# LayerNorm statistics from sums taken in the residual additions and squares taken on ScalarE, transposed inputs from the host, and a new order on every engine, in a fused attention and feed-forward block

## The chip, the cores and the metric

The kernel runs on one core of a Trainium2 chip. The metric is the time of one execution on the device, in microseconds (us). Five engines work side by side, each through a list of its own, strictly in the order in which the program was written: TensorE (PE: matmuls and transposes), VectorE (DVE), ScalarE (ACT), GpSimd (POOL) and SyncE (SP, here only a queue that issues transfers). They wait for each other through semaphores.

## What is computed

One block on x of 2 sequences x 2048 tokens x 256 channels, all float32. First linear attention with 16 heads of 16 channels, then a feed-forward layer whose inputs and weights are rounded to a block format (32 neighbours share the exponent of the largest, with 3 bits of mantissa). A LayerNorm without weights follows each.

```python
qkv = x @ Wqkv.T + bqkv;  q, k, v = split(qkv)
q, k = elu(q * scale) + 1, elu(k * scale) + 1
ksum, kvsum = cumsum(k), cumsum(k * v)            # along the tokens
y = q * kvsum / clip(sum_of_head(q * ksum), 1e-3)
x = layernorm(x + y @ Wproj.T + bproj)            # first norm, over 256 channels
h = gelu(quant(x) @ quant(w_fc).T + b_fc)         # 1024 hidden
x = layernorm(x + quant(h) @ quant(w_proj).T + b_proj)   # second norm
```

## The kernel before

The 4096 tokens are cut into 8 chunks of 512 tokens (4 tiles of 128), numbered n = 0 to 7 with the two sequences in turn. Everything is written out by hand: for each engine there are small functions, one for each step of a chunk, and a list of calls that is that engine's order. Four steps of the lists are written as a function step(s), the first and the last chunks are written out. Nothing reorders at run time.

**Attention of a chunk.** x_sb holds the chunk with tokens on the partitions. PE transposes it through a bank of PSUM (transpose_x, L1106), ACT copies it to xT (copy_xT, L512), and PE projects (project, L1116) six times, for q, k and v with two halves c of the channels. A projection goes to one of the two banks abank[0] and abank[1]. ACT takes q and k through a Relu and an Exp (activate, L521 and L523), DVE adds and takes the maximum (feature, L782), multiplies k and v (multiply_kv, L789) and runs the two cumulative sums (sum_k L794, sum_kv L799). Only then is the bank free again. POOL multiplies q by the sums (L349, L353). PE sums by head (denominators, L1127), DVE takes the reciprocal, ACT widens it (widen_rec, L531), PE transposes it (L1135), DVE forms y (attention_out, L811), PE projects it out (project_out, L1146 and L1148), DVE adds x (residual_1, L815).

**First norm.** DVE reads r1 again with bn_stats, one instruction for each tile (L821), combines them with bn_aggr (L825), and takes the negative mean (L828) and the variance plus epsilon (L829). POOL raises that to the power -1/2 (L358) and multiplies by the mean (L360). ACT applies both (norm_1, L536).

**Feed-forward of a chunk.** DVE takes the largest of each 32 (x_exponents, L834), POOL scales and rounds (L365), DVE scales back (quantise_x, L758). A transposing transfer turns it (turn_xq on SP). PE multiplies by w_fc, two halves for each tile, into the banks hbank[0] and hbank[1] (up, L1182 and L1184), and ACT applies GELU (L527). DVE takes the maxima (h_exponents, L857, L750, L753), POOL rounds (round_h, L380), DVE scales back (quantise_h, L758), a transposing transfer turns it (turn_hq), PE multiplies by w_proj into the one bank dbank (down, L1189 and L1193), DVE adds (residual_2, L869). The second norm is as the first, and SP stores the chunk.

Attention of chunk n + 2 is mixed with the feed-forward of chunks n and n + 1. The weights are loaded, q and k parts of Wqkv are scaled, and all are transposed on PE and copied on ACT at the beginning; the feed-forward weights are rounded there too (w_exponents L766, round_w L390).

[...] Exp and Gelu are in different sets, and the compiler puts an ACT_TABLE_LOAD ahead of an activation whose set isn't the one loaded. Relu, Identity, Copy and Square need none.

## Time and profile before

| | |
|---|---|
| time, median of 3 | 276.79 us (276.34 to 281.1) |
| span of the profiled execution | 273.3 us |
| median less span | 3.5 us |
| PE busy | 240.0 us, 88% |
| DVE busy | 238.9 us, 87% |
| POOL busy | 155.0 us, 57% |
| ACT busy | 151.0 us, 55% |
| granted PE clock, mean | 0.982 |
| read from and written to HBM | 7.35 MB, 4.19 MB |

The time of the profiled execution is not known by itself; its span, from the first to the last instruction, is 3.5 us under the median of the timed runs, and that difference is what lies around the span. Busy time is the time in which an engine has at least one instruction under way, so overlaps of neighbours are counted once. A mean of one instruction counts them again: the step from the start of one to the start of the next is shorter than the duration.

### The profile page before, as it was taken

The page shows a single profiled execution, that of the slowest core. Times are in us where ns is not written, and L with a number is a line of the kernel's source. Part 1 is how long each engine was busy: PE and PEld are TensorE (multiplying, and loading weights), DVE is VectorE, ACT ScalarE, POOL GpSimd, SP SyncE. Part 2 cuts the span into 40 slices and gives each one's busy share as a digit, 9 for nine tenths or more (in the row PEclk, how much of TensorE's full clock was granted, in tenths as well). Part 3 has the DMA queues.
Part 4 walks back from the last instruction along what each step waited for, and adds up shares of the span by engine and source line. Part 5 has one row for each costly group of instructions (what it writes and reads, how often), then busy time and mean ns, then how long its engine had stood idle before and what let it go on. Part 6 is the DMA issues. An engine that isn't in the chain of part 4 may idle for free.

```text
span 273.3 us, 3668 instructions
## 1 busy us (share of the span) xinstructions
PE 240.0 (88%) x1204; PEld 143.4 (52%) x1204; DVE 238.9 (87%) x513; ACT 151.0 (55%) x246; POOL 155.0 (57%) x118
## 2 busy tenths in 40 slices
PE   7999889997999899989999899989999989838761
PEld 7546636653566446644656356644664455524340
DVE  1398997998998999899989999899989997978962
ACT  2663277745556851855475754685285646332823
POOL 1076466575376656476566737675647656655851
PEclk9999999999999999999999999999999997979997
DMA  6940020036202473227304490238224530642022
GB/s 155 365 97 2 0 78 1 2 70 155 46 0 38 77 193 42 38 39 190 81 0 77 114 160 0 41 64 205 38 36 44 110 83 0 65 90 78 0 79 77
DMA packets 49474, 20.70 MB, mean 76 GB/s; under 512 B 38960, under 2 KB 49200, under 8 KB 49456
## 3 DMA queue, kind: packets, MB, share of 16 engines
q1 hardware_dynamic: 47824, 20.20, 32.7%
q10 hardware_dynamic: 1632, 0.27, 0.6%
q8 instruction: 10, 0.16, 0.3%
q14 instruction: 8, 0.07, 0.1%
HBM read 7.35 MB, written 4.19 MB: 42 GB/s over the span
## 4 chain that ended last, share of the span: by engine, by line
DVE 56%; PE 25%; DMA 8%; POOL 4%; issue 3%; ACT 2%; SPq 1%; ACTq 0%; POOLq 0%; DVEq 0%
DVE vbank L857 12%; PE abank L1116 8%; DVE hq L758 7%; DVE vbank L821 6%; PE dbank L1193 5%; DVE kvsum L799 4%; DMA h<-in_L_ffn_w_fc_dram 4%; POOL h_round L380 3%; PE hbank L1184 3%; DVE r L815 3%; DVE r L869 3%; DVE vbank L834 3%; DMA xqT<-xq 2%; DVE h_pow L750 2%; DVE kf L782 2%
## 5 line engine op out<-in xcount | busy, mean ns | idle before, releaser
L1116 PE MATMUL abank<-xT,WqkvT 128*128 128x512 f32 x176 | 81.6, 599 | 3.6 <-DVE kf L782 2.2
L380 POOL TENSOR_TENSOR h_round<-h,h_inv 128x1024 f16<-128x1024 f32 x32 | 66.5, 2079 | 31.2 <-DVE h_inv L753 28.5
L527 ACT ACTIVATE h<-hbank 128x512 f32<-128x512 f32 x64 | 36.7, 595 | 51.3 <-PE hbank L1184 51.0
L1116 PEld LDWEIGHTS abank<-xT,WqkvT 128*128 128x128 f32 x176 | 31.1, 190 | 36.2 <-issue 23.7
L857 DVE TENSOR_REDUCE vbank<-h 128x32 f32<-128x1024 f32 x32 | 39.1, 1221 | 1.6 <-ACT h L527 1.5
L349 POOL TENSOR_TENSOR qk<-qf,ksum 128x512 f32<-128x512 f32 x16 | 23.5, 1469 | 29.4 <-DVE ksum L794 18.6
L1184 PE MATMUL hbank<-w_fcT,xqT 128*128 128x512 bf16 x128 | 39.1, 387 | 0.0
L521 ACT ACTIVATE expz<-abank,zbias_neg 128x512 f32<-128x512 f32 x30 | 20.6, 687 | 31.9 <-PE abank L1116 31.4
L1193 PE MATMUL dbank<-w_prT,hT 128*128 128x256 bf16 x256 | 34.4, 279 | 1.9 <-DMA hT<-hq 1.3
L1148 PE MATMUL bbank<-WprojT,y 128*128 128x256 f32 x128 | 32.0, 380 | 0.0
L1193 PEld LDWEIGHTS dbank<-w_prT,hT 128*128 128x128 bf16 x256 | 25.2, 100 | 9.5 <-issue 3.3
L1182 PE MATMUL hbank<-bias_rows,ones_k 128*128 128x512 bf16 x64 | 25.1, 392 | 2.1 <-DMA xqT<-xq 0.9
L358 POOL TENSOR_TENSOR rstd<-vareps,minus_half 128x4 f32<-128x4 f32 (+1 forms) x18 | 17.4, 966 | 15.9 <-DVE vareps L829 15.8
L758 DVE TENSOR_TENSOR hq<-h_round,h_pow 128x1024 bf16<-128x1024 f16 x32 | 21.8, 685 | 3.5 <-POOL h_round L380 3.5
L1148 PEld LDWEIGHTS bbank<-WprojT,y 128*128 128x128 f32 x128 | 21.8, 190 | 5.2
L353 POOL TENSOR_TENSOR num<-qf,kvsum 128x512 f32<-128x512 f32 x16 | 20.9, 1324 | 5.0 <-DVE kvsum L799 5.0
L365 POOL TENSOR_TENSOR x_round<-x,x_inv 128x1024 f16<-128x1024 f32 (+1 forms) x9 | 15.5, 1723 | 13.7 <-DVE x_inv L753 13.7
L821 DVE BATCH_NORM_STATS2 vbank<-r 128x6 f32<-128x256 f32 x64 | 22.7, 420 | 0.3
L794 DVE TENSOR_TENSOR_SCAN ksum<-vbank,ksum,kf 128x512 f32<-128x512 f32 x16 | 20.5, 1279 | 0.3
L523 ACT ACTIVATE expz<-expz 128x512 f32<-128x512 f32 x32 | 20.1, 630 | 0.9
L799 DVE TENSOR_TENSOR_SCAN kvsum<-vbank,kvsum,kv 128x512 f32<-128x512 f32 x16 | 20.2, 1262 | 0.0
L1189 PE MATMUL dbank<-bias_rows,ones_k 128*128 128x256 bf16 x32 | 9.1, 283 | 12.6 <-DVE r L869 12.6
(102 smaller groups left out, 357.4 us busy)
## 6 DMA issues: line engine op xcount, KB each, us to landing
x_sb<-in_L_attn_x_dram SPq DMA_DIRECT2D x8, 512.0 KB, 3.9
out_dram<-o_sb SPq DMA_DIRECT2D x7, 512.0 KB, 3.5
h<-in_L_ffn_w_fc_dram SPq DMA_DIRECT2D x1, 1024.0 KB, 9.6
h<-in_L_ffn_w_proj_dram SPq DMA_DIRECT2D x1, 1024.0 KB, 11.1
Wqkv_sb<-in_L_attn_Wqkv_dram SPq DMA_DIRECT2D x3, 256.0 KB, 6.3
out_dram<-o_sb SPq DMA_DIRECT2D x4, 128.0 KB, 1.7
hT<-hq SPq DMA_TRANSPOSE x28, 3.1
Wproj_sb<-in_L_attn_Wproj_dram ACTq DMA_DIRECT2D x1, 256.0 KB, 7.2
```

Source lines behind the costliest of these rows:

```text
L349: nc.gpsimd.tensor_tensor(qk[:, c], qf[:, c], ksum[:, b, c], ALU.mult).then_inc(s_qk, 1)
L380: nc.gpsimd.tensor_tensor(h_round[:, t % 2].rearrange("p (g j) -> p g j", j=BLOCK_K), h[:, t].rearrange("p (g j) -> p g j", j=BLOCK_K), h_ ...
L527: nc.scalar.activation(h[:, t, half * HALF:(half + 1) * HALF], hbank[half][:, :], ACT.Gelu).then_inc(s_h, 1)
L758: return nc.vector.tensor_tensor(dst.rearrange("p (g j o) -> p g j o", j=pairs, o=2), src.rearrange("p (g j o) -> p g j o", j=pairs, o=2), ...
L799: nc.vector.tensor_tensor_scan(kvsum[:, b, c], one.broadcast_to([P, TOK]), kv[:, c], kvsum[:, b, c, TOK - 1:TOK], ALU.mult, ALU.add).then_ ...
L821: last = nc.vector.bn_stats(stats[:, t], r[:, t])
L857: nc.vector.tensor_reduce(h_amax[:, t], h[:, t].rearrange("p (g j) -> p g j", j=BLOCK_K), AX_X, ALU.max, apply_absolute_value=True).then_i ...
L1116: last = nc.tensor.matmul(ps[:, :], WqkvT[:, k, e * P:(e + 1) * P], xT[:, k], start=(k == 0), stop=(k == CC - 1))
L1148: last = nc.tensor.matmul(dst, y[:, c, t * P:(t + 1) * P], WprojT[:, c], start=False, stop=(c == CC - 1))
L1182: nc.tensor.matmul(hbank[half][:, :], ones_k[:, :], bias_rows[:, cols], start=True, stop=False)
L1184: last = nc.tensor.matmul(hbank[half][:, :], xqT[:, t, c], w_fcT[:, c, cols], start=False, stop=(c == CC - 1))
L1193: last = nc.tensor.matmul(down_ps, hT[:, slot, c], w_prT[:, c], start=False, stop=(c == HC - 1))
```

## The change

Four things change together.

1. **Sums in the additions.** residual_1 becomes four scalar_tensor_tensor instructions on 256 columns, where two tensor_tensor on 512 were, and residual_2 four where four were; each also gives the sum of its output (accum_out). One small instruction turns the sums into the negative mean. bn_stats, bn_aggr and the variance leave DVE.
2. **Squares on ACT.** For each tile ACT takes Square(r - mean) with accum_out, 64 instructions on 128x256 in all; POOL adds the epsilon with one more small instruction and goes on as before.
3. **Transposed inputs.** The host hands x, Wqkv and Wproj over transposed as well. xT comes by 8 transfers of 512 KB into two buffers; x_sb is still loaded for the residual. The transposes of x and of these weights on PE, and their copies on ACT, are gone. The scaling of the q and k weights is on DVE, in place.
4. **New orders.** All five lists are written out with other orders, without step(s). r2 has two buffers. Waits that the new orders need are written out.

```diff
             def residual_1(n, b, g):
+                wait(dve, s_mean1, n)
                 wait(dve, s_proj, 2 * n + g + 1)
-                nc.vector.tensor_tensor(r1[:, 2 * g:2 * g + 2].rearrange("p t c -> p (t c)"), bbank[1 - g][:, :],
-                                        x_sb[:, b, 2 * g:2 * g + 2].rearrange("p t c -> p (t c)"), ALU.add).then_inc(s_r1, 1)
-
-            def mean_var(done, ts, r, stats, mv, negmean, vareps, s_r, n_r, s_st, s_mv, s_ve):
+                for t in (2 * g, 2 * g + 1):
+                    last = nc.vector.scalar_tensor_tensor(r1[:, t], bbank[1 - g][:, (t % 2) * C:(t % 2 + 1) * C], 1.0, x_sb[:, b, t],
+                                                          ALU.mult, ALU.add, accum_out=sum1[:, t:t + 1])
+                last.then_inc(s_r1, 1)
+
+            def mean(done, ts, total, negmean, s_r, n_r, s_mean):
                 wait(dve, s_r, n_r)
-                for t in range(ts.start, ts.stop):
-                    last = nc.vector.bn_stats(stats[:, t], r[:, t])
-                last.then_inc(s_st, 1)
-                wait(dve, s_st, done)
-                for t in range(ts.start, ts.stop):
-                    last = nc.vector.bn_aggr(mv[:, t], stats[:, t])
-                last.then_inc(s_mv, 1)
-                wait(dve, s_mv, done)
-                nc.vector.tensor_scalar(negmean[:, ts], mv[:, ts, 0], -1.0, None, ALU.mult)
-                nc.vector.tensor_scalar(vareps[:, ts], mv[:, ts, 1], LN_EPS, None, ALU.add).then_inc(s_ve, 1)
+                nc.vector.tensor_scalar(negmean[:, ts], total[:, ts], -1.0 / C, None, ALU.mult).then_inc(s_mean, 1)
...
-                nc.vector.tensor_tensor(r2[:, t], down_ps, x1[:, b, t], ALU.add).then_inc(s_r2, 1)
...
+                nc.vector.scalar_tensor_tensor(r2[:, S % 2, t], down_ps, 1.0, x1[:, b, t], ALU.mult, ALU.add, accum_out=sum2[:, t:t + 1]).then_inc(s_r2, 1)
...
+            def squares_of(ts, r, negmean, deviation, squares, s_sq):
+                for t in range(ts.start, ts.stop):
+                    last = nc.scalar.activation(deviation[:, t], r[:, t], ACT.Square, bias=negmean[:, t:t + 1], accum_out=squares[:, t:t + 1])
+                last.then_inc(s_sq, 1)
...
+                wait(pool, s_sq, done)
+                nc.gpsimd.tensor_scalar(vareps[:, ts], squares[:, ts], 1.0 / C, LN_EPS, ALU.mult, ALU.add).then_inc(s_ve, 1)
...
+            def load_xT(n):
+                for a in range(3):
+                    wait(sp, s_qkv[a], 2 * n - 2)
+                sp.dma_start(xT[:, n % 2], xt_d[n % 2, n // 2]).then_inc(s_xT[n % 2], 16)
...
+            def scale_wqk(part):
+
+                lo = (C, 0)[part]
+                dve.wait_ge((s_wk, s_wq_in)[part], 16)
+                nc.vector.tensor_scalar(WqkvT[:, :, lo:lo + C], WqkvT[:, :, lo:lo + C], scale_sb[:, 0:1], None, ALU.mult).then_inc(s_wT, 1)
```

The order of ACT in the repeated step before, from the last GELU of a chunk to the next chunk's first (expz are Relu and Exp of attention, x<- the first norm, h<- GELU):

```order
L527 ACTIVATE h<-hbank 128x512
L521 ACTIVATE expz<-abank,zbias_neg 128x512
L523 ACT_TABLE_LOAD
L523 ACTIVATE expz<-expz 128x512
L521 ACTIVATE expz<-abank,zbias_neg 128x512
L523 ACTIVATE expz<-expz 128x512
L536 ACTIVATE x<-r,shift,rstd 128x256 x4
L521 ACTIVATE expz<-abank,zbias_neg 128x512
L523 ACTIVATE expz<-expz 128x512
L521 ACTIVATE expz<-abank,zbias_neg 128x512
L523 ACTIVATE expz<-expz 128x512
L527 ACT_TABLE_LOAD
```

And of ACT now, at the end of the feed-forward of chunk 3 and the beginning of that of chunk 4:

```order
L565 COPY rec_wide<-rec 128x1024
L553 ACTIVATE expz<-abank,zbias_neg 128x512
L555 ACT_TABLE_LOAD
L555 ACTIVATE expz<-expz 128x512
L560 ACT_TABLE_LOAD
L560 ACTIVATE h<-hbank 128x512
L553 ACTIVATE expz<-abank,zbias_neg 128x512
L555 ACT_TABLE_LOAD
L555 ACTIVATE expz<-expz 128x512
L560 ACT_TABLE_LOAD
L560 ACTIVATE h<-hbank 128x512
L575 ACTIVATE deviation,squares<-r,negmean 128x256 x4
```

The four Relu and Exp pairs of a chunk stood together, with two table loads for a chunk; now most stand singly between GELUs, each with a load ahead of its Exp and one behind it. The whole ACT list has 34 loads, and it had 14.

The order of DVE in the repeated step before, around the second norm's statistics:

```order
L869 TENSOR_TENSOR r<-dbank,x 128x256
L799 SCALAR_TENSOR_TENSOR kvsum<-vbank,kvsum,kv 128x512
L821 BN_STATS vbank<-r 128x6 x4
L825 BN_AGGR vbank<-vbank 128x2 x4
L828 TENSOR_SCALAR negmean<-vbank 128x4
L829 TENSOR_SCALAR vareps<-vbank 128x4
```

And of DVE now, where the attention of chunk 4 and the feed-forward of chunk 2 end:

```order
L915 SCALAR_TENSOR_TENSOR r,sum<-bbank,x_sb 128x256 x4
L921 TENSOR_SCALAR negmean<-sum 128x4
L966 SCALAR_TENSOR_TENSOR r,sum<-dbank,x 128x256
L921 TENSOR_SCALAR negmean<-sum 128x4
L853 TENSOR_TENSOR hq<-h_round,h_pow 128x1024
```

Ten instructions of statistics for a chunk's norm have become one, and the additions carry the sums. On PE, the transposes of x (L1106) stood between the projections and the matmuls of the feed-forward:

```order
L1116 MATMUL abank<-xT,WqkvT 128x512 x2
L1106 MATMUL abank<-ident,x_sb 128x128 x4
L1189 MATMUL dbank<-bias_rows,ones_k 128x256
L1193 MATMUL dbank<-w_prT,hT 128x256 x8
L1106 MATMUL abank<-ident,x_sb 128x128 x4
```

And now, between the last `up` of chunk 1 and the first of chunk 2, with projections of chunks 4 and 5 between them:

```order
L1331 MATMUL hbank<-bias_rows,ones_k 128x512
L1333 MATMUL hbank<-w_fcT,xqT 128x512 x2
L1262 MATMUL abank<-xT,WqkvT 128x512 x4
L1331 MATMUL hbank<-bias_rows,ones_k 128x512
L1333 MATMUL hbank<-w_fcT,xqT 128x512 x2
```

They are gone from the list. The projections stand three chunks ahead of the feed-forward, where they stood two ahead: five of the six of chunk 2 now stand ahead of the first `up` of chunk 0, and before only half a transpose of chunk 2 did.

## Rows read from the trace of the kernel before

**Rows 1.** The page: busy time by engine; the chain that ended last, by engine.
```profile
PE 240.0 (88%) x1204; PEld 143.4 (52%) x1204; DVE 238.9 (87%) x513; ACT 151.0 (55%) x246; POOL 155.0 (57%) x118
DVE 56%; PE 25%; DMA 8%; POOL 4%; issue 3%; ACT 2%; SPq 1%; ACTq 0%; POOLq 0%; DVEq 0%
```
**Rows 2.** Windows: length, then each engine's busy time (and instructions), clock, DMA.
```profile
12.50:34.60 22.10, 20.50 (x96) 12.40 (x95) 20.93 (x30) 9.33 (x15) 12.76 (x6) 1.00 0.19 52
124.58:154.15 29.57, 27.83 (x138) 16.53 (x137) 28.19 (x61) 17.87 (x29) 18.05 (x14) 1.00 0.34 80
243.40:273.30 29.90, 17.81 (x126) 10.04 (x124) 19.43 (x54) 13.35 (x26) 13.95 (x14) 0.90 0.20 62
```
**Rows 3.** Waits from 124.58 to 154.15: who waited for whom, total, times, longest.
```profile
ACT h L527 <- PE hbank L1184: 7.4, 4, 3.4
PE dbank L1189 <- DVE r L869: 1.0, 1, 1.0
DVE hq L758 <- POOL h_round L380: 0.6, 1, 0.6
```
**Rows 4.** Timeline of DVE in the same step: start, length, instruction.
```profile
128.77 0.42 DVE L869 TENSOR_TENSOR r<-dbank,x 128x256 f32<-128x256 f32 x1
129.10 1.27 DVE L799 TENSOR_TENSOR_SCAN kvsum<-vbank,kvsum,kv 128x512 f32<-128x512 f32 x1
130.29 0.73 DVE L782 SCALAR_TENSOR_TENSOR kf<-abank,zbias,expz 128x512 f32<-128x512 f32 x1
130.93 0.68 DVE L758 TENSOR_TENSOR xq<-x_round,x_pow 128x1024 bf16<-128x1024 f16 x1
...
136.04 1.39 DVE L821 BATCH_NORM_STATS2 vbank<-r 128x6 f32<-128x256 f32 x4
137.47 0.41 DVE L825 BATCH_NORM_AGGREGATE vbank<-vbank 128x2 f32<-128x6 f32 x4
...
138.06 0.21 DVE L804 TENSOR_SCALAR den<-bbank 128x64 f32<-128x64 f32 x1
```
**Rows 5.** Timeline of PE in the same step.
```profile
132.89 0.60 PE L1106 MATMUL abank<-ident,x_sb 128*128 128x128 f32 x4
133.33 0.27 PE L1189 MATMUL dbank<-bias_rows,ones_k 128*128 128x256 bf16 x1
```
**Rows 6.** Groups of the whole run: busy us, mean ns | idle before.
```profile
L815 DVE TENSOR_TENSOR r<-bbank,x_sb 128x512 f32<-128x512 f32 x16 | 10.9, 684 | 0.0
L527 ACT ACTIVATE h<-hbank 128x512 f32<-128x512 f32 x64 | 36.7, 595 | 51.3 <-PE hbank L1184 51.0
L521 ACT ACTIVATE expz<-abank,zbias_neg 128x512 f32<-128x512 f32 x30 | 20.6, 687 | 31.9 <-PE abank L1116 31.4
L523 ACT ACTIVATE expz<-expz 128x512 f32<-128x512 f32 x32 | 20.1, 630 | 0.9
L531 ACT COPY rec_wide<-rec 128x1024 f32<-128x1024 f32 x8 | 8.3, 1041 | 2.8 <-DVE rec L806 2.4
L496 ACT ACTIVATE table<-minus_half 128x4 f32<-128x4 f32 x1 | 0.2, 206 | 0.0
```
**Rows 7.** Timeline of ACT: an Exp with its table load, and a norm's four instructions.
```profile
149.33 0.69 ACT L521 ACTIVATE expz<-abank,zbias_neg 128x512 f32<-128x512 f32 x1 [1.12 <-PE abank L1116]
150.03 1.28 ACT L523 ACT_TABLE_LOAD   x1
151.33 0.63 ACT L523 ACTIVATE expz<-expz 128x512 f32<-128x512 f32 x1
...
153.29 2.06 ACT L536 ACTIVATE x<-r,shift,rstd 128x256 f32<-128x256 f32 x4
```
**Rows 8.** Timeline near the start, and two rows at the end.
```profile
12.52 2.29 DVE L766 TENSOR_REDUCE vbank<-h 128x64 f32<-128x2048 f32 x1 [2.98 <-DMA h<-in_L_ffn_w_fc_dram]
...
268.86 0.15 DVE L829 TENSOR_SCALAR vareps<-vbank 128x2 f32<-128x2 f32 x1
269.09 0.69 POOL L358 TENSOR_TENSOR rstd<-vareps,minus_half 128x2 f32<-128x2 f32 x1 [2.45 <-DVE vareps L829]
```

1227 lines of the change are left out of this document (726 added, 501 removed).

## Prediction

> **What bounds the kernel now.** I read the page's busy times and the chain that ended last first: PE is busy for 88% of the span and DVE for 87%, and the chain runs for 56% over DVE and 25% over PE [rows 1]. The two are too near each other for an average, so the windows come next. The middle of the run repeats a step of 29.57 us for each chunk. In it DVE is busy for 28.19 us, PE for 27.83, POOL for 18.05 and ACT for 17.87 [rows 2]. The waits of that step tell who waits for whom: PE's longest is for DVE's residual_2, 1.0 us, DVE's longest is 0.6 us for POOL, and ACT's 7.4 us for PE are the slack of an idle engine [rows 3]. So in the middle DVE sets the time, PE would be late next at 27.8, and ACT and POOL have over 11 us to spare. The ends differ: in the last 29.9 us DVE is busy for 19.43 and PE for 17.81, at a clock of 0.90 [rows 2]. There the waits from one engine to the next decide.
>
> **DVE.** A norm's statistics go from 136.04 to 138.06 [rows 4], 2.02 us for each of two norms: minus 4.0 a chunk. One small instruction in place of them, with its wait, is 0.2 us, twice: plus 0.4. The additions become dearer. residual_2 took a step of 0.33 us (128.77 to 129.10) for 256 columns [rows 4]; residual_1 lasts 0.684 us for 512 [rows 6], 0.60 as a step if it overlaps its neighbour by the same 0.09. Together 4 x 0.33 + 2 x 0.60 = 2.5 us. Now they are eight scalar_tensor_tensor on 256 columns. That form takes a step of 0.64 for 512 (130.29 to 130.93) [rows 4], 0.04 over the plain addition, and I take 0.40 for 256 with that and rounding up. No row shows a sum written out beside the output. Its price lies between nothing and 0.27 us, what 256 columns more would cost (0.60 less 0.33). I take 0.08, the step of the smallest instruction of statistics, four in 0.41 us [rows 4], since it writes one column. So 8 x 0.48 = 3.8 us, and DVE's balance is -4.0 + 0.4 - 2.5 + 3.8 = -2.3 us a chunk (-2.9 with free sums, -0.8 at the upper end). From 28.8 (28.19 and its own gaps) it comes to 26.5.
>
> [...]
>
> **PE.** A transpose of half a chunk's x takes 0.44 us (132.89 to 133.33) [rows 5]. Two go: -0.9 us a chunk, from 27.8 to 26.9. Without DVE's statistics PE is now the later of the two.
>
> **ACT.** It loses two copies of x, some 1.2 us a chunk, and gains eight squares and many table loads. From the first GELU of chunk 0 to the last of chunk 5 I counted its new list: 49 GELUs of 0.595, 21 pairs of Relu and Exp of 0.687 + 0.630, 6 widenings of 1.04 [rows 6], 44 norm instructions and 46 squares of 2.06 / 4 = 0.515, and 33 table loads of 1.28 [rows 7]. That is 29.2 + 27.7 + 6.2 + 22.7 + 23.7 + 42.3 = 151.8 us. The 46 sums cost between nothing and 0.206 us each, the smallest activation [rows 6]. I take 0.1, since neighbours overlap: 4.6, so 156.4 (152 to 161). The same stretch holds some 5.55 chunks' work of DVE, 147 us (143 to 155), and 5.35 of PE, 144 us. **ACT becomes the longest of three level engines there**, and what makes it so is the loads: with 2 a chunk, some 12 in the stretch, it would have 130.
>
> A load's price is well seen: Relu ends at 150.02, the load starts at 150.03 and the Exp at 151.33 [rows 7]. [...]
>
> **POOL** gets one small instruction a norm, 0.2 us by its like: from 18.1 to 18.5 a chunk, with 8 to spare. **SP** issues 8 more transfers of 512 KB, moved ahead of transposing transfers at some places; DMA is busy for 0.34 of the step [rows 2], and some 4 MB more are hidden behind a double buffer. I cost both at nothing; a turned tile that comes 1 us late would cost that in its chunk.
>
> **The beginning.** DVE still starts on weights that arrive at 12.52 [rows 8], and is then busy for 20.93 of the next 22.1 us [rows 2], so its list sets this part too. Before its first maxima of h it now has 11 features and 6 products of k and v at 0.64, 11 cumulative sums at 1.19 [rows 4], four products y at 0.60, and two maxima of weights (2.29 each [rows 8], 3.1 with their small ones), 2.4 for two roundings, and some 6 of the rest: 41.0 us. With 2.7 of waiting for the first norm, which is now a longer chain (DVE, ACT, POOL, ACT), it gets there at 56; the first GELU is 3 us earlier, at 53. More of chunk 2 is then behind it. The earlier projections alone buy nothing, as DVE's start is tied to the weights.
>
> **The end.** Behind the last GELU of chunk 5 DVE has some 31 us of its list left. From its last instruction to the end of the span it was 273.3 - 269.0 = 4.3 us [rows 8]; two squares with their sums and one more step on POOL in place of the variance make 5.7. With 3 of waits (before, chunk 7's feed-forward stood alone; now it is mixed with chunk 6's) 39.5.
>
> **The sum.** 53 + 156.4 + 4.5 (the waits of the longest engine in the middle, 3%; DVE's were 1.4 of 29.6) + 39.5 = 253.4 us of span, 20 under 273.3. The median stands 3.5 above the span: **257 us**, 7% less.
>
> **Rivals.**
> - *ACT isn't felt* (0.15). If the squares' sums are free and loads fall into gaps, DVE and PE set the middle at 147 to 149: 53 + 149 + 38 + 3.5 = 243.5 us. For it: before, ACT waited 7.4 us of a step for PE. Against it: it has 151.8 us of work without any wait.
> - *The loads break the hand-over* (0.14). A projection waits for its bank, and that for Relu, load, Exp and feature. Where a pair stands singly, both loads lie between PE's projection and its next use of hbank or abank. If 1 us of each of the 16 extra round trips is lost to all: 257 + 16 = 273 us, no difference.
> - *The loads rule* (0.06), slower. The same mechanism, on PE's in-order list, at its full price. To reach 282 the middle must take 186 us, 42 over PE's 144: 2.6 us in each of the 16 trips, which is both loads bare. That would be so where PE has nothing between such projections that doesn't need ACT. With Relu, Exp and feature laid bare as well (2.0 us) it would be 16 x 4.6 = 74, and 314 us. Against it: two banks, and matmuls of `down` between. A switch that idles ACT beyond the load's own record would do the same without PE: for 282 us it would take 25 us over 33 loads, 0.76 us each, where the rows show 0.02. Of the 0.06 this has 0.01. [...]
> - *It doesn't do what it says*: a sum costs a second pass (0.27 us). 64 x 0.19 = 12 us on DVE, of which 8 lie under ACT: 261, inside the forecast.
>
> **Chances.** The forecast, 246 to 264, has 0.65. The range reaches from 245 to 271: it takes in the unknown sums, most of the lossy hand-over, and leaves out some 0.08 below and 0.12 above. A measurement of this kernel tells about 2% from no change (271.3 to 282.3). Faster: 0.84, same: 0.10, slower: 0.06.
>
> **What would show it.** In the new trace: no more than 26.9 us of PE a chunk; ACT's busy time near 205 us (before 151.0) with 34 loads; additions of some 0.46 us; ACT's waits for PE down from 51 us for GELU to under 20; DVE's idle time in the middle up to 2 a chunk; the first GELU near 53. It is wrong if the sums cost more than 0.3 us, if ACT's rows show gaps around loads, or if PE waits for features for over 1 us a projection.

## The result, and the profile after

The changed kernel takes 301.9 us in the median (300.4 to 303.8), the kernel before 277.0 us beside it: a ratio of 1.089 with a 95% interval of 1.082 to 1.097. Some executions of a kernel are slower at a lower granted clock (278.6 us at 0.966 for the kernel before, beside its median of 276.5 at 0.975); the medians here are over all executions, and the intervals of the ratios leave the slow ones out. The forecast was 257 us, so it was wrong in sign and by 45 us. The profiled execution has a span of 299.1 us against 273.3.

The page of the changed kernel first: busy time by engine, the granted clock of TensorE in 40 slices, and the chain that ended last.

```profile
PE 236.6 (79%) x1124; PEld 141.0 (47%) x1124; DVE 241.5 (81%) x449; ACT 197.7 (66%) x374; POOL 153.9 (51%) x136
...
PEclk9599869999999997999869997999999997979997
...
PE 35%; DVE 30%; issue 11%; ACT 9%; DMA 8%; POOL 3%; SPq 2%; DVEq 0%; ACTq 0%; POOLq 0%
```

Against [rows 1], ACT's busy time grew as planned, PE's fell a little. DVE was to lose some 18 us and is at 241.5, above the 238.9 of before, with 64 instructions fewer. Something in DVE's list lasts longer than it did. Grouping the list by line and shape shows what (busy us, mean ns of one | idle before):

```profile
L853 DVE TENSOR_TENSOR hq<-h_round,h_pow 128x1024 bf16<-128x1024 f16 x32 | 28.1, 882 | 1.3 <-POOL h_round L408 1.3
L848 DVE TENSOR_SCALAR h_inv<-h_pow 128x32 uint16<-128x32 uint16 x32 | 11.0, 344 | 1.1
L853 DVE TENSOR_TENSOR xq<-x_round,x_pow 128x1024 bf16<-128x1024 f16 x7 | 9.2, 1316 | 0.3 <-issue 0.3
L921 DVE TENSOR_SCALAR negmean<-sum 128x4 f32<-128x4 f32 x14 | 9.0, 641 | 0.8
```

The product `xq` takes 0.68 us in [rows 4] and 1.32 on average here. Its counterpart `hq` has the same size. A mean over four numbers takes 0.64 us. The timeline shows where the time goes: one stretch of DVE, POOL and PE in the middle, by engine.

```profile
143.34 3.92 POOL L408 TENSOR_TENSOR h_round<-h,h_inv 128x1024 f16<-128x1024 f32 x2
148.14 2.28 POOL L394 TENSOR_TENSOR x_round<-x,x_inv 128x1024 f16<-128x1024 f32 x1 [0.88 <-DVE x_inv L848]
...
143.51 0.23 DVE L845 TENSOR_SCALAR h_pow<-vbank 128x64 uint16<-128x64 uint16 x1
143.77 1.51 DVE L848 TENSOR_SCALAR h_inv<-h_pow 128x32 uint16<-128x32 uint16 x1
...
147.97 0.68 DVE L853 TENSOR_TENSOR hq<-h_round,h_pow 128x1024 bf16<-128x1024 f16 x1
148.57 0.42 DVE L966 SCALAR_TENSOR_TENSOR r<-dbank,x 128x256 f32<-128x256 f32 x1
148.91 2.05 DVE L853 TENSOR_TENSOR hq<-h_round,h_pow 128x1024 bf16<-128x1024 f16 x1
150.88 0.74 DVE L880 SCALAR_TENSOR_TENSOR qf<-abank,zbias,expz 128x512 f32<-128x512 f32 x1
...
144.01 0.59 PE L1333 MATMUL hbank<-w_fcT,xqT 128*128 128x512 bf16 x2
151.68 3.47 PE L1262 MATMUL abank<-xT,WqkvT 128*128 128x512 f32 x4 [7.07 <-DVE qf L880]
```

What to see: `h_inv` at 143.77 starts inside POOL's first rounding and ends at 145.28, where the first of the two roundings ends (half of 3.92 us on from 143.34). The second `hq` starts at 148.91 inside POOL's `x_round`, which ends at 150.42, and ends itself at 150.96, where 0.69 us alone would have been enough. Instructions between them that read or write PSUM (`h_pow`, the addition `r`) keep their length. PE has waited 7.07 us for the bank that `qf` frees. Of the lateness of `qf` some 2.7 us are the stretching (1.33 of `h_inv`, 1.37 of `hq`), an estimate from their lengths. The rest is the order: the Exp that `qf` reads had ended at 147.18, and DVE had six other instructions to end before `qf`. Then PE runs four products in 3.47 us, half of the rate of the 1.88 us for four that it has elsewhere: the granted clock in these 3.47 us is 0.56.

This is no single case. In the changed kernel 35 of the instructions `hq`, `xq`, `h_inv`, `x_inv` and `negmean` start while a multiplication of POOL (a rounding, `qk` or `num`) is under way, and all 35 end behind it: the small ones by 0.02 to 0.04 us, the products of 1024 columns by 0.55 us, or 0.62 where one started in the multiplication's last 0.1 us. In the kernel before only 5 start so, four `h_inv` (up to 0.59 us, from 0.18) and one `hq`.

So `hq` takes 0.68 us undisturbed and up to 2.25 behind a multiplication of POOL. What ties the two engines together no row shows; which instructions it lengthens, and by how much, the rows do. The prediction did not reckon with it, though the trace of before had signs of it in those four `h_inv`, and in POOL's rounding, which takes 1.90 us, or 2.28 where `hq` starts just ahead of it:

```profile
122.35 0.68 DVE L758 TENSOR_TENSOR hq<-h_round,h_pow 128x1024 bf16<-128x1024 f16 x1
122.52 2.28 POOL L380 TENSOR_TENSOR h_round<-h,h_inv 128x1024 f16<-128x1024 f32 x1 [0.32 <-DVE h_inv L753]
```

Last, the three parts that the prediction added up: length, busy time of PE, PEld, DVE, ACT and POOL, clock, DMA. The first part ends with the first GELU, the second with the last GELU of chunk 5.

```profile
0.00:62.60 62.60, 51.92 (x197) 29.58 (x198) 43.06 (x74) 25.79 (x45) 24.04 (x23) 0.89 0.36 110
62.60:241.00 178.40, 150.95 (x713) 90.57 (x711) 156.04 (x290) 142.80 (x260) 99.44 (x84) 0.96 0.32 76
241.00:299.10 58.10, 33.72 (x216) 20.90 (x216) 42.43 (x88) 29.16 (x71) 30.42 (x30) 0.90 0.35 78
```

Forecast were 53, 160.9 and 39.5 us. All three are longer, by 9.6, 17.5 and 18.6 us. For the sum of the stretching I took, for the groups of DVE that were seen stretched, the length above the undisturbed 0.685 (`hq`, `xq`), 0.416 (half `xq`), 0.181 (`h_inv`, `x_inv`) and 0.16 us (`negmean`): 29.5 us in the changed kernel (0.6 in the beginning, 18.3 in the middle, 10.6 in the end), and 0.9 us in the kernel before.

### The profile page after: what moved, and what is told of

Same layout as the page of the kernel before. It is cut to its first block, busy times and chain, and to the rows that moved or that the text cites. A ratio compares the mean times of both kernels' runs of the same rounds, so it can differ in the third digit from the quotient of the medians.

```text
span 299.1 us, 3876 instructions
## 1 busy us (share of the span) xinstructions
PE 236.6 (79%) x1124; PEld 141.0 (47%) x1124; DVE 241.5 (81%) x449; ACT 197.7 (66%) x374; POOL 153.9 (51%) x136
## 4 chain that ended last, share of the span: by engine, by line
PE 35%; DVE 30%; issue 11%; ACT 9%; DMA 8%; POOL 3%; SPq 2%; DVEq 0%; ACTq 0%; POOLq 0%
PE abank L1262 13%; PE bbank L1296 7%; DVE vbank L951 6%; ACT deviation L575 5%; DVE hq L853 4%; PE dbank L1343 3%; PE hbank L1333 3%; PE bbank L1274 3%; DMA xqT<-xq 3%; DMA hT<-hq 3%; DVE vbank L927 2%; DMA WqkvT<-in_WqkvT_dram 2%; PE hbank L1262 2%; PE hbank L1331 2%; DVE r L966 2%
## 5 line engine op out<-in xcount | busy, mean ns | idle before, releaser
L1262 PE MATMUL abank<-xT,WqkvT 128*128 128x512 f32 x176 | 86.6, 620 | 12.9 <-DVE qf L880 7.1
L408 POOL TENSOR_TENSOR h_round<-h,h_inv 128x1024 f16<-128x1024 f32 x32 | 63.4, 1982 | 41.4 <-DVE h_inv L848 39.0
L1262 PEld LDWEIGHTS abank<-xT,WqkvT 128*128 128x128 f32 x176 | 33.2, 199 | 46.7 <-issue 25.5
L560 ACT ACTIVATE h<-hbank 128x512 f32<-128x512 f32 x64 | 36.8, 593 | 17.1 <-PE hbank L1333 16.5
L575 ACT ACTIVATE deviation<-r,negmean 128x256 bf16<-128x256 f32 x64 | 31.7, 496 | 22.7 <-DVE negmean L921 22.6
L1343 PE MATMUL dbank<-w_prT,hT 128*128 128x256 bf16 x256 | 35.3, 283 | 5.4 <-DMA hT<-hq 4.4
L1296 PE MATMUL bbank<-WprojT,y 128*128 128x256 f32 x128 | 36.5, 419 | 0.0
L853 DVE TENSOR_TENSOR hq<-h_round,h_pow 128x1024 bf16<-128x1024 f16 x32 | 28.1, 882 | 1.3 <-POOL h_round L408 1.3
L380 POOL TENSOR_TENSOR num<-qf,kvsum 128x512 f32<-128x512 f32 x16 | 20.7, 1291 | 15.5 <-DVE kvsum L897 11.8
L1296 PEld LDWEIGHTS bbank<-WprojT,y 128*128 128x128 f32 x128 | 24.8, 216 | 6.4 <-issue 1.5
L966 DVE SCALAR_TENSOR_TENSOR r<-dbank,x 128x256 f32<-128x256 f32 x32 | 13.3, 416 | 11.2 <-PE dbank L1343 11.1
L385 POOL TENSOR_SCALAR vareps<-squares 128x4 f32<-128x4 f32 (+1 forms) x18 | 3.9, 219 | 33.7 <-ACT deviation L575 33.5
```

The source lines that it names most:

```text
L408: nc.gpsimd.tensor_tensor(h_round[:, t % 2].rearrange("p (g j) -> p g j", j=BLOCK_K), h[:, t].rearrange("p (g j) -> p g j", j=BLOCK_K), h_ ...
L560: nc.scalar.activation(h[:, t, half * HALF:(half + 1) * HALF], hbank[half][:, :], ACT.Gelu).then_inc(s_h, 1)
L575: last = nc.scalar.activation(deviation[:, t], r[:, t], ACT.Square, bias=negmean[:, t:t + 1], accum_out=squares[:, t:t + 1])
L853: return nc.vector.tensor_tensor(dst.rearrange("p (g j o) -> p g j o", j=pairs, o=2), src.rearrange("p (g j o) -> p g j o", j=pairs, o=2), ...
L1262: last = nc.tensor.matmul(ps[:, :], WqkvT[:, k, e * P:(e + 1) * P], xT[:, n % 2, k], start=(k == 0), stop=(k == CC - 1))
L1296: last = nc.tensor.matmul(dst, y[:, c, t * P:(t + 1) * P], WprojT[:, c], start=False, stop=(c == CC - 1))
```

## The experiments

The change has three parts: statistics by sums and squares, transposes from the host, and the new lists. Four runs asked first which part loses and whether the table loads do. The kernel before ran between them and took 276.5 us, and 276.4 to 276.8 beside all the later ones. Times are medians, with the interval of the ratio to the kernel before.

**The statistics alone, in the old order.** DVE adds with `accum_out` and takes `mean`; ACT's list gets the squares where a turn seemed free; POOL's list has the root one place later.

```diff
-                nc.vector.tensor_tensor(r2[:, t], down_ps, x1[:, b, t], ALU.add).then_inc(s_r2, 1)
+                nc.vector.scalar_tensor_tensor(r2[:, t], down_ps, 1.0, x1[:, b, t], ALU.mult, ALU.add, accum_out=sum2[:, t:t + 1]).then_inc(s_r2, 1)
...
                 activate(n, 1, 0, abank[0])
+                n = s + 1
+                squares_1(n)
+                n = s + 2
                 activate(n, 0, 0, abank[1])
...
+                n = s + 1
+                round_h(n, 0)
                 n = s
                 scale_shift_2(n)
                 n = s + 1
-                round_h(n, 0)
                 round_h(n, 1)
```

> The kernel before with only the new statistics: sums in the residual additions, squares on ScalarE, one small instruction more on GpSimd; the old order, transposes on the chip, and one r2. Two places had to move so that GpSimd doesn't stand waiting: squares_1 stands behind the first Relu and Exp pair of a step, squares_2 where norm_2 stood with norm_2 two GELUs later, and scale_shift stands one rounding later. ACT keeps its 14 table loads. Theory A (the new order is what costs; the statistics help as forecast, -2.3 us of DVE a chunk): 255 to 265 us. Theory B (the longer chain DVE, ACT, GpSimd, ACT of a norm is what costs): 280 us or more. Theory C (small DVE instructions on SBUF wait for GpSimd's long ones): A's gain less up to 1.2 us a mean, 262 to 272 us, with means of over 0.3 us in the trace.

Measured: 291.2 us, ratio 1.047 to 1.061. The statistics lose 14.7 us by themselves, though DVE's busy time falls from 238.9 to 222.8 us. The timeline of one first norm, DVE then ACT then POOL:

```profile
123.02 0.42 DVE L864 SCALAR_TENSOR_TENSOR r<-bbank,x_sb 128x256 f32<-128x256 f32 x1
123.48 1.06 DVE L870 TENSOR_SCALAR negmean<-sum 128x4 f32<-128x4 f32 x1
...
125.29 0.69 ACT L527 ACTIVATE expz<-abank,zbias_neg 128x512 f32<-128x512 f32 x1 [1.58 <-PE abank L1161]
127.83 0.49 ACT L547 ACTIVATE deviation<-r,negmean 128x256 bf16<-128x256 f32 x1
129.80 0.66 ACT L527 ACTIVATE expz<-abank,zbias_neg 128x512 f32<-128x512 f32 x1
...
131.57 2.08 ACT L542 ACTIVATE x<-r,shift,rstd 128x256 f32<-128x256 f32 x4 [0.45 <-POOL shift L366]
...
122.24 2.28 POOL L386 TENSOR_TENSOR h_round<-h,h_inv 128x1024 f16<-128x1024 f32 x1 [0.39 <-DVE h_inv L800]
...
129.98 0.19 POOL L362 TENSOR_SCALAR vareps<-squares 128x4 f32<-128x4 f32 x1 [1.47 <-ACT deviation L547]
```

The last addition ends at 123.44, the squares start at 127.83 and ACT's normalisation follows at 131.57, 8.13 us behind the addition; before it was 4.8 to 5.1 us. The mean is stretched (1.06 us) by POOL's rounding, which ends at 124.52, the squares wait for their turn in ACT's list, and the second Relu and Exp of the chunk stand behind the squares. Theory B is borne out (over 280 us), and theory C in its means of over 0.3 us.

**The host's transposes alone, in the old order.**

```diff
-            transpose_x(0, 0, 0, abank[0])
...
-            copy_xT(0, 0, abank[0])
...
+            load_xT(2)
```

> The kernel before with only the transposed inputs from the host: no transposes of x and of the attention weights on TensorE, no copies of them on ScalarE, the scaling of the q and k weights on VectorE, xT by transfers into two buffers; the old order otherwise. Theory A (DVE sets the middle, so 0.9 us of PE a chunk is hidden): 272 to 278 us. Theory B (the start is late: the loads come in another sequence, and TensorE idles and loses its clock before the first projection): 277 to 283 us, with a granted clock under 1 before 20 us.

Measured: 280.9 us, 1.010 to 1.026. The steps are no slower (29.50 us a chunk against 29.64, from the first GELUs of the steps); the first GELU comes at 50.05 us and not at 46.82. The granted clock from 20 to 40 us is 0.83, where it was 1.00, behind a wait of PE:

```profile
23.10 2.82 PE L1086 MATMUL bbank<-headmask,qk 128*128 128x8 f32 x16 [4.04 <-POOL qk L355]
```

The transposes that went had kept PE busy there. The first step is 1.4 us longer too (30.93 us against 29.51), so that the second chunk's first GELU is 4.65 us late. The total is 4.4 us longer, so the loss lies ahead of that GELU.

**The changed kernel without its switches of tables**: Exp is replaced by a second GELU, so the attention's features are not the reference's.

```diff
-                nc.scalar.activation(expz[:, a, c], expz[:, a, c], ACT.Exp, scale=-1.0).then_inc(s_z[a], 1)
+                nc.scalar.activation(expz[:, a, c], expz[:, a, c], ACT.Gelu, scale=-1.0).then_inc(s_z[a], 1)
```

> The changed kernel with Gelu in place of Exp in the attention's activation, so that no table is switched: part of the computation is changed, all durations but the 33 loads of 1.28 us (42 us on ACT) stay. Theory A (the loads in the hand-over of PSUM banks and in the queue of ACT are what costs): 302 falls to 270 or lower. Theory B (DVE is the bound, lengthened by waits behind GpSimd, and the order makes PE and DVE wait for each other): under 10 us of gain, 292 or more. Between them both hold their share.

Measured: 303.5 us, 1.087 to 1.119. ACT's busy time falls from 197.7 to 156.9 us, and DVE's (241.4) and POOL's (153.9) stay. The 32 loads of 1.28 us that are gone, of 34, cost nothing in this kernel. The rival *the loads rule* and its milder form are out here; whether loads would be felt once the stretching is gone was not tried.

**The changed kernel with the sums in PSUM.**

```diff
-        sum1 = sb("sum1", [P, TILES])
-        sum2 = sb("sum2", [P, TILES])
+        sum1, sum2 = vbank[:, 296:300], vbank[:, 304:308]
```

> The changed kernel with sum1 and sum2 in the spare PSUM bank that the old statistics used, nothing else. Theory C (a DVE instruction that reads and writes only SBUF waits until a GpSimd instruction under way has ended): the 18 means fall from 10.5 us to 3 us in all, the time by 3 to 8 us. Theory B without C: no change within 1%, and the means stay long.

Measured: 298.7 us, 1.067 to 1.089, some 3 us less than the changed kernel. The means are back at 0.16 us (from 0.64 and 0.39), 7.6 us less of them, while the other stretched groups stay as they were:

```profile
L920 DVE TENSOR_SCALAR negmean<-vbank 128x4 f32<-128x4 f32 x14 | 2.3, 164 | 0.8
```

DVE's busy time falls by 4.4 us only (to 237.1), since the read of a sum takes 141 ns into PSUM and 81 into SBUF.

**Both parts in the old order.** The edits are those of the first two kernels together.

```diff
+                squares_1(n)
...
+                load_xT(n)
```

> The old order of every engine with both other parts of the change in it: sums and squares on ScalarE, and the transposes from the host. Alone in the old order they gave 291.2 us (+14.7) and 280.9 us (+4.4) against 276.5. If the two are independent: about 295.6 us, and the new order is left with some 6 of the 25 us that the change loses. If the new order is what loses (a theory that the runs so far only weaken): 290 us or less here, the two parts overlapping in the same idle time. If the new order gains something back: over 302 us here.

Measured: 289.1 us, 1.037 to 1.050. So the two overlap (14.7 and 4.4 us stood alone, and together they cost 12.6), and the new order costs 12.8 us of the 25. The same grouping as above, of this kernel, shows that the order makes most of the stretching, 12.1 us in all here against 29.5:

```profile
L784 DVE TENSOR_TENSOR hq<-h_round,h_pow 128x1024 bf16<-128x1024 f16 x32 | 21.8, 685 | 3.7 <-POOL h_round L392 3.7
L849 DVE TENSOR_SCALAR negmean<-sum 128x4 f32<-128x4 f32 x14 | 10.8, 775 | 0.2
L779 DVE TENSOR_SCALAR h_inv<-h_pow 128x32 uint16<-128x32 uint16 x32 | 7.6, 238 | 1.1
L784 DVE TENSOR_TENSOR xq<-x_round,x_pow 128x1024 bf16<-128x1024 f16 x7 | 4.8, 684 | 0.0
```

In the old order DVE's products start ahead of POOL's next rounding or after the last one has ended, so they keep their 0.685 us. The new instructions, the means, fall into POOL's time (10.3 of the 12.1 us), and a few of `h_inv` (1.8).

**Earlier squares, in the old order**: the first norm's ahead of the first Exp, the second's behind the first GELU of the next chunk.

```diff
-                activate(n, 1, 0, abank[0])
...
                 squares_1(n)
...
+                activate(n, 1, 0, abank[0])
                 activate(n, 0, 0, abank[1])
...
                 gelu(n, 0, 0)
+                n = s
+                squares_2(n)
+                n = s + 1
                 gelu(n, 0, 1)
```

> The statistics alone in the old order, as before in 291.2 us, but ScalarE's four squares stand one or three instructions earlier in its list: the first norm's before the first Exp of the chunk after, where ScalarE idled 1.58 us, the second norm's after the first GELU of the next chunk, where it idled 1.75 us. Nothing else differs. Theory of the hand-over (what costs is the way from the last addition over mean, squares and POOL back to ScalarE, 8.13 us there against 5.05 us before, in which the squares waited 3.3 us for their turn): the period of a chunk falls from 31.5 us by 1 to 2 us, and the time to 277 to 284 us. Theory of the stretched VectorE instructions (those that touch only SBUF and run while POOL multiplies): unchanged, 289 to 292 us. A theory of ScalarE's load (the 12 us of reads and 32 us of squares as such, wherever they stand): unchanged too.

Measured: 289.4 us, 1.040 to 1.052. Only 1.8 us came back, less than the theory of the hand-over asked. The squares now start 1.14 us behind the addition, but the root stands at 5.43 us, since POOL has a rounding of 2.28 us ahead of it; and `kf` waits for the Exp that the squares delay (14.3 us in all, from 6.6 with the later squares). Part of what one side gained the other took.

**The changed kernel with one short square a norm**, so without the variance.

```diff
-                for t in range(ts.start, ts.stop):
-                    last = nc.scalar.activation(deviation[:, t], r[:, t], ACT.Square, bias=negmean[:, t:t + 1], accum_out=squares[:, t:t + 1])
+                for t in range(ts.start, ts.start + 1):
+                    last = nc.scalar.activation(deviation[:, t, 0:8], r[:, t, 0:8], ACT.Square, bias=negmean[:, t:t + 1], accum_out=squares[:, t:t + 1])
```

> The changed kernel with one square of 8 columns in place of four (or two) of 256 for each norm, so it leaves out the variance: the other columns keep a constant set at the start. Waits and order stay, and VectorE's sums and means too. ScalarE has some 32 us of squares less and each hand-over is about 2 us shorter. Theory of the hand-over or of ScalarE's load: 16 hand-overs, of which those that the next step waits for fall by 2 us: 288 to 294 us. Theory of the stretched VectorE instructions, or of the new order as such: 299 to 303 us.

Measured: 290.1 us, 1.037 to 1.051. The squares cost 11.8 us of 301.9, and not all of it need be their own length: with the instructions shifted against each other, DVE's stretching is 23.6 us here, 5.9 less.

**The changed kernel with the old statistics.**

```diff
-                mean(n + 1, ALL, sum1, negmean1, s_r1, 2 * n + 2, s_mean1)
+                mean_var(n + 1, ALL, r1, stats1, mv1, negmean1, vareps1, s_r1, 2 * n + 2, s_st1, s_mv1, s_ve1)
```

> The changed kernel, its order and the host's transposes kept, with the statistics of the kernel before: VectorE's batch-norm pass in the place of the means, no sums, no squares, plain additions. VectorE has about 4 us more a chunk, ScalarE some 32 us less in all. If the statistics on ScalarE are what loses, in this order as in the old one: 280 to 288 us. If the new order (with the start) is what loses: 297 to 305 us, since VectorE has more to do in a list that already made others wait. If the order was laid out for short statistics, both hold: 288 to 297 us.

Measured: 307.6 us, 1.104 to 1.116. The new order with the old statistics is the slowest of all. DVE is busy for 257.5 us in it, 18.6 more than in the kernel before, with the same instructions and two that scale weights (1.0 us). Its products are stretched as in the changed kernel (`hq` 878 ns, `xq` 1077), 17.4 us of stretching in all. In this order the new statistics gain 5.7 us; in the old one they lose 14.7.

**No shared reads, in the changed kernel**, a name for what the run takes away: of the instructions of DVE that were seen stretched none reads two operands from SBUF, or goes from SBUF to SBUF, any more, but for the two products of the weights in the beginning. What is left out stands in the expectation.

```diff
-                nc.vector.tensor_scalar(inv.bitcast(U16), pow2.bitcast(U16)[:, :, 0], -1.0, float(TO_GRID),
+                nc.vector.tensor_scalar(inv.bitcast(U16), top[:, :, 0], -1.0, float(TO_GRID),
...
-                times_power(hq[:, t], h_round[:, t % 2], h_pow[:, t], HB).then_inc(s_hq, 1)
+                by_one(hq[:, t], h_round[:, t % 2]).then_inc(s_hq, 1)
...
+                return nc.vector.tensor_tensor(dst[:, 0:n], src[:, 0:n], one.broadcast_to([P, n]), ALU.mult)
```

> The changed kernel with the sums in PSUM (298.7 us so), and with the other VectorE instructions that touched only SBUF beside POOL's multiplications replaced by ones of the same length that read one SBUF operand at most: the products hq and xq by a product of 600 (or 300, of a half) of the 1024 columns with a constant 1 from PSUM, and the inverse exponents read from the maxima in PSUM and not from h_pow. So the scaling back by the powers is left out, the other columns stay zero, and the mantissa bits stay in the inverse. Order, waits and lengths of undisturbed instructions (0.69 and 0.18 us) are kept. In the changed kernel the means of hq, xq, h_inv and x_inv were 0.88, 1.32, 0.34 and 0.45 us, against 0.69, 0.68, 0.24 and 0.18 in the old order, some 20 us in all. Theory that the new order loses by such stretched instructions: hq back at 0.69, VectorE busy 217 us in place of 237, and 280 to 290 us. Theory that the order loses by its waits and its start alone: 296 to 300 us.

Measured: 284.3 us, 1.024 to 1.033. That is 14.4 us less than with the sums in PSUM alone and 17.6 less than the changed kernel, in the middle of the expected span. The lengths of the three parts are 63.5, 170.5 and 49.7 us, where the changed kernel has 62.6, 178.4 and 58.1. POOL's 32 roundings of h are all back at 1.90 us too. The replacements are even a little longer than the undisturbed instructions:

```profile
L858 DVE TENSOR_TENSOR hq<-h_round,vbank 128x600 bf16<-128x600 f16 x32 | 24.8, 778 | 1.0 <-POOL h_round L407 1.0
L847 DVE TENSOR_SCALAR h_inv<-vbank 128x32 uint16<-128x32 uint16 x32 | 6.1, 191 | 1.1
```

**The same in the old order, as a control**, with the same edit.

```diff
+                by_one(hq[:, t], h_round[:, t % 2]).then_inc(s_hq, 1)
```

> The control: the same replacement, leaving out the same parts, in the old order with both other parts of the change (289.1 us). There only the means were stretched (0.78 us each of 14 against 0.16). Theory of the stretched instructions: VectorE busy 224 us falls by 11 us at most, and the time by 0 to 4 us, to 285 to 289 us, since the means' lateness (1.1 us) is the only part on a path that others wait for. If this kernel falls as far as the changed one, the replacement has an effect of its own and proves nothing.

Measured: 285.9 us, 1.029 to 1.041, 3.2 us less and not 17.6, so the replacement has no large effect of its own. Without shared reads the two orders are alike (284.3 and 285.9 us), so the 12.8 us that the new order costs are what DVE's products and inverses lose beside POOL's multiplications: the 32 `hq` last 0.88 us on average in the changed kernel and 0.685 in the old order with both parts, the 32 `h_inv` 0.34 and 0.24. POOL's 32 roundings of h are longer in both orders than the 1.90 us that they take here, but no more so in the new one (1.98 us, and 2.09 in the old).

**The statistics in the old order at their best**: earlier squares, sums in PSUM, POOL's list of before.

```diff
-                n = s + 1
-                round_h(n, 0)
                 n = s
                 scale_shift_2(n)
                 n = s + 1
+                round_h(n, 0)
                 round_h(n, 1)
```

> The statistics alone in the old order with the earlier squares (289.4 us), the sums in PSUM, and POOL's list as in the kernel before (the reciprocal roots ahead of the next rounding of h, not behind it). With the earlier squares the first norm was 6.88 us behind the last addition: mean at 1.1, squares 1.14 to 3.2, but the root at 5.43, since POOL had a rounding of 2.28 us ahead of it. Theory of the hand-over: mean at 0.2, squares from 0.3 to 2.3, root at 2.5, first norm at 3.9, sooner than the 5.05 of the kernel before, and with VectorE some 4 us a chunk shorter 268 to 278 us. If ScalarE's squares in the step before Exp are what costs (Exp waits behind them, and the features behind Exp): 282 to 290 us.

Measured: 286.9 us, 1.035 to 1.042. Mean, squares and root are where they were expected (0.26, 0.30 and 2.74 us), but the normalisation comes 6.03 us behind the addition, as ACT has two pairs of Relu and Exp and a table load ahead of it, and `kf` waits for ACT:

```profile
123.64 0.49 ACT L546 ACTIVATE deviation<-r,negmean 128x256 bf16<-128x256 f32 x1
124.14 0.67 ACT L526 ACTIVATE expz<-abank,zbias_neg 128x512 f32<-128x512 f32 x1
...
126.78 0.75 DVE L829 SCALAR_TENSOR_TENSOR kf<-abank,zbias,expz 128x512 f32<-128x512 f32 x1 [2.05 <-ACT expz L528]
```

The theory of the hand-over fell here, as stated; the one of the squares in ACT's turn stands.

**The host's transposes with PE kept busy.**

```diff
             project(0, 2, 1, dbank)
+            for _ in range(16):
+                nc.tensor.transpose(abank[0][:, 0:P], ident[:, :], ident[:, :])
```

> The host's transposes alone in the old order (280.9 us), with 16 transposes of the identity into a free bank in the 4.04 us that TensorE waited from 19.1 us on. In that kernel the wait was followed by 16 small products in 2.82 us (1.85 at the full clock), a projection in 3.76 us (1.9) and transposes in 1.73 (1.1), the granted clock 0.83 in 20 to 40 us, and the first GELU came 3.2 us later than before. Theory that the clock after this wait is the cost: granted clock near 1.00 there, first GELU 2 to 3 us sooner, 277 to 279 us. Theory that the later start is DMA or VectorE: no change, 280 to 282 us.

Measured: 282.0 us, 1.009 to 1.023: no gain, and inconclusive. The first GELU came at 47.62 us in the profiled execution, 2.4 sooner, and the clock from 20 to 40 us was 0.91. That fits the clock behind the wait as the cause of the later start, though it is one execution, the slowest of the four (283.7 us); whether the clock explains the end time stays open.

**Which norm.** One kernel with sums for the second norm only, one for the first only; the other norm keeps `bn_stats`. Both start from the kernel of 286.9 us; the edit shown is that of the first.

```diff
-                mean_1(n)
+                mean_var_1(n)
```

> The kernel before, with sums and squares for the second norm only (the sums in PSUM, the four squares behind the first GELU of the next chunk, where ScalarE idled), and the batch-norm pass kept for the first. VectorE, which bounds the kernel before, is some 2 us a chunk shorter, and of the second norm only the store and the next chunk's second additions wait. Theory that the loss comes through the first norm and the Exps behind its squares: 268 to 276 us, perhaps the fastest of all. Theory that the squares delay the GELUs and so lose wherever they stand: 278 to 284 us.

> The counterpart: sums and squares for the first norm only, as placed in the kernel of 286.9 us, and batch norm for the second. Theory that the loss comes through the first norm: 282 to 288 us, though VectorE is 2 us a chunk shorter here too. If the loss of the two is half and half: 279 to 283 us.

Measured: 283.0 us (1.019 to 1.029) and 281.3 us (1.013 to 1.021). By the total it looks like half and half, but the period of a chunk tells them apart. It is taken from ACT's timeline, as the mean distance between the first GELUs of chunks 1 to 6:

| kernel | period, us | DVE busy, us | time, us |
|---|---|---|---|
| before | 29.64 | 238.9 | 276.6 |
| second norm only | 29.71 | 226.2 | 283.0 |
| first norm only | 30.17 | 226.3 | 281.3 |
| both norms | 30.27 | 214.4 | 286.9 |
| both norms, short squares | 28.51 | 214.1 | 275.3 |

The last row is the kernel of the next experiment. In these steps the second norm costs nothing (29.71 against 29.64 us), and the first 0.5 us in each. The first norm also makes the step of chunk 0 2.2 us longer (31.76 us against 29.51). DVE's 12.7 us less bring nothing in either. The second norm's 6.3 us are lost behind the steps, where POOL waits for the squares of chunk 6 with the roundings of chunk 7 behind it:

```profile
256.18 0.19 POOL L363 TENSOR_SCALAR vareps<-squares 128x4 f32<-128x4 f32 x1 [6.16 <-ACT deviation L555]
```

**Both norms, short squares**, in the old order (the variance is left out): the short square of above, in the kernel of 286.9 us.

```diff
+                for t in range(ts.start, ts.start + 1):
+                    last = nc.scalar.activation(deviation[:, t, 0:8], r[:, t, 0:8], ACT.Square, bias=negmean[:, t:t + 1], accum_out=squares[:, t:t + 1])
```

> The kernel of 286.9 us (both norms by sums, early squares, sums in PSUM, POOL's old list) with one square of 8 columns a norm in place of four or two of 256: the variance is left out, the other columns keep a constant. The first norm's squares then end some 1.6 us sooner and the Exp behind them starts as much sooner. Theory of ScalarE's squares in the chain: the period of 30.3 us falls below the 29.7 us of the kernel before, and the time to 266 to 275 us. If something else of the statistics costs (the sums, the means, POOL's extra instruction): 280 us or more.

Measured: 275.3 us, 0.992 to 0.999. The squares cost 11.6 us here, as many as in the new order (11.8), and without them the period is 28.51 us. The stretching is the same in both (2.3 us), so it has no part in these 11.6.

**Both taken away in the changed kernel.**

```diff
+                by_one(hq[:, t], h_round[:, t % 2]).then_inc(s_hq, 1)
...
+                for t in range(ts.start, ts.start + 1):
```

> The changed kernel with both taken away: no shared reads as in e9 (284.3 us; leaves out the scaling back by the powers and 424 of 1024 columns of the products) and one short square a norm as in e7 (leaves out the variance). Separately they gave 17.6 and 11.8 us of 301.9. If they add up: 272 to 275 us. If they overlap, both ending in the same waits: 278 to 283 us. The forecast of the changed kernel was 257 us; what is left above it belongs to the start (first GELU at 63 us, not 53), the clock and the list itself.

Measured: 280.0 us (276.0 to 283.4) over ten executions, 278.7 over the six that the interval of 1.001 to 1.011 rests on. They overlap: 22 to 23 us together, where 17.6 and 11.8 stood alone. So these two make up nearly the whole 25 us that the change lost against the kernel before; what is left, 22 to 23 us above the forecast, is the gain that did not come.

**The end mended.** In two more kernels POOL rounds two tiles of chunk 7 before the root of chunk 6; the same edit is made in the kernel with sums for the second norm only and in the one for both.

```diff
-            scale_shift_2(6)
             round_h(7, 0)
             round_h(7, 1)
+            scale_shift_2(6)
```

> As the kernel with sums for the second norm only (282.9 us), with one entry of POOL's list moved: the reciprocal root of chunk 6's second norm behind the first two roundings of h of chunk 7. POOL waited 6.16 us for it there, and the roundings behind it came some 4 us later than in the kernel before (257.7 against 253.8 us). If that wait is the whole loss: 275 to 278 us, the same as before (276.6), and VectorE's 12.7 us less are worth nothing in the steps. If the shorter VectorE gains anything: below 274 us.

> The same move in the kernel with both norms by sums, early squares, sums in PSUM and POOL's old list (286.9 us), where POOL's longest wait for squares was 7.3 us. Its period of a chunk was 30.3 us against 29.7 before, some 4 us over the seven steps. If the end and the period are the two parts of the 10.4 us: 280 to 283 us.

Measured: 279.5 us (1.008 to 1.014) and 285.0 us (1.028 to 1.034). The move gave 3.4 and 1.9 us. The wait was not the whole loss of 6.3 us. The kernel with the second norm only has a period of 29.70 us, but from its last step on it takes 53.1 us (277.6 - 224.5) against 48.8: the last GELUs of chunk 7 start 2.45 us later, behind the squares of chunk 6. No kernel with sums that computes the whole is faster than the kernel before.

## Why the prediction was wrong

**What bounds it.** "In the middle DVE sets the time" was the first error, though a small one in the sum. DVE was the busiest and its busy time was near the period [rows 2], but with 12.7 us taken from it the period stayed (29.71 against 29.64), and with 24.8 us and short squares it fell by 1.1 us a chunk only. What bounds the step instead I infer and have not shown: a circle of hand-overs from PE over ACT, DVE and POOL back to PE, each in its fixed order, in gaps of which DVE's statistics stood.

**The middle, 156.4 + 4.5 us.** It was 178.4. The sum took the longest list, ACT's at 156.4 us, with 4.5 us of waits. Both terms failed. The longest list was DVE's, busy for 156.0 us, as near to 156.4 as it is by luck: DVE's was forecast at 147. Less the 18.3 us of stretching it is 137.7, below my 147, as the sums were cheaper than I took: the step of an addition with its sum is 0.35 us (0.33 without), not 0.48.

This is the step of the prediction that failed: DVE's list was priced by durations from rows in which `hq`, `xq`, `h_inv` and the small instructions stood clear of POOL, for a list that no longer keeps them clear. The stretching was put at nothing; it measured 29.5 us over the whole kernel, and taking the shared reads away gave 17.6 us of time.

The 4.5 us of waits were the other half of it. Of the 178.4 us DVE was idle for 22.4, PE (busy for 151.0) for 27.4 and ACT for 35.6. No engine was the bound by its sum, and in the least idle of them stood 4.0 us of gaps a chunk (22.4 / 5.55), where up to 2 were foreseen.

**ACT, 156.4 us.** Its list was 142.8 us long. The squares with their sums took 22.0 us (44 of them, where I had counted 46) and not 28.3, since the sums hid in the steps of the squares (0.49 us each, the read of 188 ns inside), and the GELUs took 24.3 against 29.2, since neighbours overlap (one lasts 0.60 us, two in a row 1.09). Its busy time of 197.7 us against 205 and the 34 loads are near the forecast, and the waits for PE in front of GELU fell to 16.5 us as forecast. ACT did not become the longest engine, as its list was shorter than forecast and DVE's longer; in the middle it waited 9.5 us for means and 11.8 for PE's projections. And yet its squares cost 11.8 us. That this is by their place between the mean and the root, and not by their sum, fits the second norm's squares, which cost nothing in the steps, but is not shown by itself.

**The table loads.** The price of 1.28 us with nothing behind it was right, and I costed them on the path, as 42.3 of ACT's 156.4 us. Without them the time is the same (303.5 against 301.9 us), as they fall into ACT's waits. The rival *the loads rule* would need 0.76 us of idle time of ACT beyond each load; behind 33 of the 34 loads the next instruction starts 0.01 us later.

**The beginning, 53 us.** It was 62.6. DVE's list between the weights and the first maxima of h took about the forecast time, 41.9 us of work from 12.68 to 64.84 where 41.0 were forecast; but it waited 10.3 us in that stretch and not 2.7. The first projection needs scaled weights that land at 8.3 us, PE is idle for 3.5 us before it, and its first projections then run at half the rate:

```profile
8.88 3.78 PE L1262 MATMUL hbank<-xT,WqkvT 128*128 128x512 f32 x4 [3.52 <-DVE WqkvT L818]
...
36.94 0.37 PE L1294 MATMUL bbank<-bias_rows,ones_k 128*128 128x256 bf16 x1 [4.02 <-DVE y L909]
```

With the shared reads gone the first GELU stays at 63.5 us, so stretching (0.6 us in this part) has no part in it. The clock was taken as in [rows 2], 1.00, and was 0.89 in this stretch.

**The end, 39.5 us.** It was 58.1. DVE's 31 us were 42.4, of which 10.6 are stretching: the list was counted rightly (31.8). The rest is 7 us more of waits of DVE than the 8.5 foreseen. PE waited in this part 4.50 and 3.52 us for the halves of `xq`, and DVE 5.1 us for PE's `down`. Without the shared reads the part took 49.7 us.

**PE, 26.9 us a chunk.** 144 us were forecast for the middle and 151.0 measured, at a granted clock of 0.96 on average. The clock accounts for it by an estimate, 144 / 0.96 = 150, which no run checks.

**The transfers, costed at nothing.** Right for the steps of the old order (29.50 us a chunk). In the new order PE's weight loads waited 6.2 us for `hT` and 5.8 for `xqT`, where they were 1.9 and 1.4 before; no experiment separates what that costs.

**The rivals.** None of them was the case. Both conditions of *ACT isn't felt* held (the sums were nearly free and the loads fell into gaps), and still the middle took 178.4 us and not 149. That a sum costs a second pass is refuted by the step of 0.35 us. The chance of 0.06 for slower went to one mechanism, the loads, that costs nothing; the mechanism that ruled stood in no rival. Of the 45 us above the forecast the runs show 22 to 23 (shared reads and squares, overlapping). The rest stays open. The beginning, 9.6 us late, is part of it, for neither removal moved its end by much (63.5 us without shared reads, 61.4 with short squares); the clock and the waits of the new list are candidates, and no run splits them.

## What to carry to other kernels

A duration read from a trace belongs to its neighbours in time as well as to its instruction (`hq` took 0.68 us clear of GpSimd's multiplications and up to 2.25 beside one): before an order is changed, mark every VectorE product of two SBUF operands, every small VectorE instruction from SBUF to SBUF and every multiplication of GpSimd, and ask which of them will now meet. That a trace shows few of them stretched says nothing of another order: 5 started inside a multiplication in the kernel before, 35 in the changed one. Putting the sums in PSUM brought the means back to 0.16 us, from 0.64 and 0.39, for 60 ns more at each read of a sum.

The busiest engine is not the bound until taking work from it has moved the period of a step. Compare periods, start and end apart; the total alone would have blamed the wrong norm here.

Moving work to an engine with idle time costs its length again where it stands between two hand-overs of the same value, and it delays what is queued behind it: the squares cost 11.6 and 11.8 us of the time in two orders, where the 24.5 us that left DVE's list (238.9 to 214.4) bought 1.3 us with the squares all but gone (275.3 against 276.6).
